# Eight products of constants on TensorE ahead of the turning of a layer norm's result

## The reference

```python
x = x + tanh(g_xattn[0]) * L0_xattn(_layernorm(x), ctx, ctx, mask, ...)   # attention, 16 heads      A0
x = x + tanh(g_ffn[0])   * L0_ffn(_layernorm(x), ...)                     # 8 experts, top 2         M0
x = x + tanh(g_xattn[1]) * L1_xattn(_layernorm(x), ctx, ctx, mask, ...)   # attention with biases    A1
x = x + tanh(g_ffn[1])   * L1_ffn(_layernorm(x), ...)                     # switched attention       SW
x = x + tanh(g_xattn[2]) * L2_xattn(_layernorm(x), ctx, ctx, ...)         # mLSTM                    ML
x = x + tanh(g_ffn[2])   * L2_ffn(_layernorm(x), ...)                     # quantised conv FFN       CF
x = x + tanh(g_xattn[3]) * L3_xattn(_layernorm(x), ctx, ctx, ...)         # one wide head, then FFN  WA
x = x + tanh(g_ffn[3])   * L3_ffn(_layernorm(x), ...)                     # 16 experts, top 4        M3
```

## Time and profile before

| | |
|---|---|
| median of three runs | 3420.51 us (3406.86 to 3446.26) |
| the profiled execution | 3412.93 us |
| its span, first to last instruction | 3410.8 us |
| TensorE busy | 2673.2 us, 78% |
| VectorE, ScalarE, GpSimd busy | 52%, 43%, 4% |
| mean granted TensorE clock | 0.789 of full |

### The profile page before, as it was taken

The page is one execution under the profiler, slowest core; times in us unless marked ns, Lnnn a source line. Parts: engine busy times, 40 slices in busy tenths (PEclk is TensorE's granted clock), DMA queues, the critical chain, the costliest instruction groups (busy, mean ns, idle before and its releaser), DMA issues.

```text
span 3410.8 us, 50340 instructions
## 1 busy us (share of the span) xinstructions
PE 2673.2 (78%) x18402; PEld 1795.5 (53%) x18402; DVE 1782.7 (52%) x6456; ACT 1466.3 (43%) x4498; POOL 138.9 (4%) x180
## 2 busy tenths in 40 slices
PE   5888688876888777887778877788778887788876
PEld 2556445654556544565445654456544564454644
DVE  4544654447544565444654347543565435744356
ACT  3363243632436324462344622446234462345622
POOL 0000000000000000000000000000000000000000
PEclk9896787876879678796788867888678886788867
DMA  2041000410004000040000500004000050000400
GB/s 118 1 100 38 7 10 1 100 38 13 4 1 115 23 13 4 7 113 18 14 2 7 118 13 14 2 7 118 13 15 2 7 118 13 15 3 19 109 10 4
DMA packets 311269, 114.93 MB, mean 34 GB/s; under 512 B 267712, under 2 KB 294336, under 8 KB 310768
## 3 DMA queue, kind: packets, MB, share of 16 engines
q1 hardware_dynamic: 311024, 111.72, 12.9%
HBM read 63.46 MB, written 48.23 MB: 33 GB/s over the span
## 4 chain that ended last, share of the span: by engine, by line
PE 55%; DVE 22%; ACT 14%; issue 5%; DMA 3%; POOL 1%; SPq 0%; DVEq 0%; ACTq 0%
PE banks L448 5%; ACT PP L772 5%; PE banks L392 5%; PE banks L327 5%; PE banks L641 3%; PE banks L514 3%; DVE nm L1087 3%; PE banks L541 3%; PE banks L330 2%; PE banks L291 2%; PE banks L601 2%; PE banks L339 2%; DVE xn L1044 2%; PE banks L487 2%; PE banks L415 2%
## 5 line engine op out<-in xcount | busy, mean ns | idle before, releaser
L772 ACT ACTIVATE PP<-banks,nm 128x128 f32<-128x128 f32 x1568 | 482.2, 380 | 226.4 <-DVE nm L1087 139.4
L1087 DVE TENSOR_REDUCE nm<-banks 128x8 f32<-128x1024 f32 (+1 forms) x208 | 240.8, 1161 | 514.6 <-PE banks L330 345.7
L780 ACT ACTIVATE PP<-banks 128x512 f32<-128x512 f32 (+1 forms) x400 | 236.5, 593 | 265.6 <-PE banks L392 258.2
L392 PE MATMUL banks<-w_sb,PP 128*128 128x128 f32 x1536 | 297.8, 328 | 33.5 <-ACT PP L772 27.0
L392 PEld LDWEIGHTS banks<-w_sb,PP 128*128 128x128 f32 x1536 | 207.0, 168 | 101.5 <-issue 46.3
L1629 POOL TENSOR_TENSOR rs<-mv,half 128x2 f32<-128x2 f32 x160 | 112.5, 703 | 2966.0 <-DVE mv L1024 2966.0
L514 PE MATMUL banks<-va,PP 128*128 128x64 f32 x1024 | 169.4, 318 | 50.8 <-ACT PP L780 41.1
L448 PEld LDWEIGHTS banks<-w_sb,qk 128*128 128x128 f32 x1280 | 193.3, 241 | 7.2 <-issue 3.1
L327 PE MATMUL banks<-qk,gs 32*128 32x512 f32 x512 | 185.7, 808 | 12.9 <-ACT PP L772 8.2
L448 PE MATMUL banks<-w_sb,qk 128*128 128x128 f32 x1280 | 192.5, 323 | 0.9 <-DVE qk L1222 0.9
L291 PE MATMUL banks<-w_sb,xn 128*128 128x128 f32 x288 | 79.0, 373 | 143.5 <-DVE xn L1044 118.9
(11 more groups left out here) (281 smaller groups left out, 5146.8 us busy)
## 6 DMA issues: line engine op xcount, KB each, us to landing
va<-v_d SPq DMA_DIRECT2D x32, 512.0 KB, 5.9
o_d<-oa SPq DMA_DIRECT2D x64, 256.0 KB, 2.1
va<-o_d SPq DMA_DIRECT2D x32, 512.0 KB, 3.9
pv_d<-PP SPq DMA_DIRECT2D x16, 512.0 KB, 4.3
oa<-pv_d SPq DMA_DIRECT2D x16, 512.0 KB, 4.3
v_d<-PP SPq DMA_DIRECT2D x16, 512.0 KB, 3.6
v_d<-tmp SPq DMA_DIRECT2D x16, 512.0 KB, 3.3
w_sb<-weights SPq DMA_DIRECT2D x1, 5603.0 KB, 22.4
```

The source lines that it names most:

```text
L392: e = pe.transpose(bank(k, 2)[:, cols(j)], P[k][:, 512 * (u % 2) + 128 * j:][:, 0:128], ident)
L772: e = act.activation(P[k][:, 512 * (u % 2) + 128 * j:][:, 0:128], bank_[:, cols(j)], ACT.Exp, bias=nm[k][:, m:m + 1], accum_out=ssum[k][:, ...
L780: act.activation(PT[k][:, 512 * (u % 2):512 * (u % 2) + maps * 128], bank(k, 2)[:, 0:maps * 128], ACT.Copy).then_inc(pT_ok[k], 1)
L1087: e = dve.tensor_reduce(m, b3(scores[:, 0:maps * 128], maps), AX.X, ALU.max, negate=True)
```

## The change

A new helper waits until x has been updated by the last stage and then runs eight bf16 products of 128x512: the identity `identb` is the stationary operand and `causb`, repeated four times, the moving one. They write the whole of the bank whose first half `pe_turn` overwrites directly afterwards. Nothing reads their result. The helper is called directly ahead of `pe_turn` in M0, A1, SW, ML, CF, WA and M3, in both lanes and all 8 turns: 7 x 2 x 8 = 112 times, 896 products. A0 and the second layer norm of WA are left as they are. Other engines' programs don't change.

```diff
+        def pe_idle_products(pe, k, i, stage, n):
+
+            pe.wait_ge(x_up[k], x_up.n(i, stage - 1))
+            for _ in range(8):
+                pe.matmul(bank(k, n), identb[:, :], bc(causb[:, :], 1, 4), start=True, stop=True, skip_group_check=True)
+
         def pe_turn(pe, k, i, j, src, n):
...
@@ pe_small_attention
             yield
+            if s:
+                pe_idle_products(pe, k, i, A1, 2)
             pe_turn(pe, k, i, (XN_A0, XN_A1)[s], xn[k], 2)
...
@@ pe_mixture0
             yield
+            pe_idle_products(pe, k, i, M0, 0)
             pe_turn(pe, k, i, XN_M0, xn[k], 0)
...
@@ pe_switched_attention
+            pe_idle_products(pe, k, i, SW, 0)
             pe_turn(pe, k, i, XN_SW, xn[k], 0)
...
@@ pe_mlstm
+            pe_idle_products(pe, k, i, ML, 0)
             pe_turn(pe, k, i, XN_ML, xn[k], 0)
...
@@ pe_conv_ffn
+            pe_idle_products(pe, k, i, CF, 0)
             pe_turn(pe, k, i, XN_CF, xn[k], 0)
...
@@ pe_wide_attention
+            pe_idle_products(pe, k, i, WA, 2)
             pe_turn(pe, k, i, XN_WA, xn[k], 2)
...
@@ pe_mixture3
+            pe_idle_products(pe, k, i, M3, 0)
             pe_turn(pe, k, i, XN_M3, xn[k], 0)
```

## The result

The changed kernel takes 3481.35 us (median of four runs, 3472.38 to 3496.68) against 3415.54 before: a ratio of 1.0174, with a 95% interval from 1.0109 to 1.024. It is slower, as forecast (3445), and inside the range, but by more: 66 us between the medians, where the forecast was 25 above the median known then. The profiled execution is the slowest of the four, 3496.68 us; its span is 3494.6 us, 83.8 more than that of the kernel before, where the prediction's sum had 33.

A forecast was written before the change was run, and what follows sets the result against it. TensorE, busy 78% of the span, was taken as nearest to the bound. Costs of 24.9 less gains of 19.8 gave 5.1 us in a turn, 41 in eight, four fifths 33; on 3412.93, 3446, said as 3445; range 3365 to 3530.

The forecast's parts named there:

- The wait on x_up costs nothing: In all fourteen places of a turn TensorE arrives after x was updated, so the new wait was costed at 0.
- The price of a product: Eight products take 1.7 us at full clock, 3.4 at half; beyond idle time, 24.9 us in a turn.
- The cover: TensorE's idle time before L291's transposes, 143.5 us, about 1 us per place, under which added products cost nothing.
- The products raise the clock: A set run at half leaves the clock at full, saving 19.8 us in a turn; mean clock 0.789 to about 0.85.
- Attention holds the clock: Behind A1 of lane 1, attention at half would run at full clock and stay there, saving 6.6 us in a turn.
- The places that I left out: Savings counted only for work right behind a set; A0 of lane 1 to M0 of lane 0 reckoned at +1.7 us.
- Four fifths of it reach the end: Later waits on TensorE may absorb delay or gain, so 33 of the 41 us in eight turns were taken.
- The first: Rival: the clock rises but attention behind A1 of lane 1 doesn't hold it; 75 us more, 3488; chance 0.22.
- The second: Rival: the products, multiplying constants, don't raise the clock, which stays at 0.79; 159 us more, 3572; chance 0.08.
- the third: Rival: CF, WA and M3 sets keep the clock full until the next set, above 0.9; 3358 us; chance 0.25.
- my own case: Products cost 24.9 us in a turn and the clock gives 19.8 back; 3400 to 3480 us, chance 0.45.

The follow-up runs named there:

- e6: The changed kernel with one product in place of eight in each of the 112 places, wait kept; 1.0026 against the kernel before.
- e3: The kernel before with the eight products in one place of a turn alone, A1 of lane 1; 0.9975 against the kernel before.
- e9: The changed kernel plus six quarter-array products ahead of the second output turning in A0 of lane 0, from the second turn on; 1.0353 against the kernel before.
- e10: The changed kernel plus six quarter-array products ahead of the first output turning in A0 of lane 0; 1.0199 against the kernel before, 3471.77 us.

## Why the prediction was right, and where it was off

- *The wait on x_up costs nothing.* Right: idle before the products 0.0, and e6 at 1.0026.
- *The price of a product.* Right: 1.73 and 3.39 us for a set, 1.7 and 3.4 reckoned. The clock at the place was not always as reckoned: the sets of A1 of lane 1 and of WA of lane 1 run at full (WA's was counted under the gains), and all sets cost 22 us in a turn beyond their cover, where 24.9 were put in.
- *The cover.* Right: of the 13.6 us of idle time in the fourteen places of the turn of the earlier trace rows, only the 0.68 before ML of lane 1 is still idle in the changed kernel's turn.
- *The products raise the clock.* Right in kind: M3 of lane 0 and WA of lane 1 show it, and quarter-array products in the same places give 1.0985 (e1). It gave less than I put in, some 15 us in a turn by the sum below and not 19.8, and the mean clock rose to 0.813 where I had named about 0.85.
- *Attention holds the clock.* It can, against the rule of the Trainium skill for transposes ("TensorE: Matmul & The Clock Gate", Part 4: PE-mode transpose) that the prediction weighed: −6.2 us reckoned as −6.6 (e3), at 1.00 in seven of eight turns. It does not always: in the changed kernel the clock falls once in that stretch (0.84), and about 4.4 us were gained behind the set of A1 of lane 1. That this row of the table came out near what was reckoned is luck: the set itself was reckoned at 3.4 us and the stretch that ends with it grew by nothing (−0.2), since its clock was higher too.
- *The places that I left out.* This is the step that was off most. The sum took for granted that "What that saves is the work right behind it", and that every other stretch keeps the clock it had. The stretch between A0 of lane 1 and M0 of lane 0 lost its full clock and cost 7.4 us in a turn where 1.7 were reckoned, 5.7 too little. All other stretches together came to +5.1, reckoned +3.4, with errors of both signs among them. So the one stretch is 5.7 of the 7.4 us by which the turn was off.
- *Four fifths of it reach the end.* Not borne out: the differences between the marks already contain whatever later waits absorb, and outside the one stretch they came to more than the full sum, not to less (+5.1 against +3.4). Turns 2 to 7 add up to 75 us, the start gives 1.5, the first turn 2 and the last 5.5, which makes the 83.8 of the profiled execution.
- *The rivals.* The first (attention doesn't hold the clock) gave 3488, near the measured 3481, by the wrong mechanism. It was a stretch without any change ahead of it that fell, not the one behind A1. The second (clock as before) and the third (above 0.9 and shorter turns) are out, with the clock at 0.813 and longer turns.

The sum that fits the profiled execution is thus: 22 us in a turn for the uncovered products (35.7 from set to transposes in the turn of the earlier trace rows, less 13.6 of cover), 5.7 lost by the clock where nothing was expected, and, as what then remains to 12.5, some 15 given back elsewhere. The 15 are not measured apart. The median, 3481, lies just above my own case (3400 to 3480); it is inside the range of 3365 to 3530 because the rivals, with other mechanisms, had widened it. That much is luck. The median of the runs is 15 us below that execution; which stretches fell in the runs without a trace stays open. It also stays open which of the thirteen other places add the last tenths of a us to the shift; only M3 of lane 1 was taken away alone.

## What to carry to other kernels

On a kernel that swings between the two clocks, price an added or moved burst in two sums: what it costs and saves on the spot, which rows give to some tenths of a us as long as the clock at the place stays what it was, and what the shift does to every later stretch that is at one clock by a narrow margin. List these stretches first (the same mixture at 1.00 in one place and 0.50 in another gives them away) and give the forecast a term for each. If products are to warm the clock, add them in few places with a long stretch behind them and test each alone; two places gave 0.988 here, three covered ones 1.004, fourteen 1.017.

## What was not expected of the hardware

- One group of full-array work raised the clock in all 63 turns in which it began up to 0.66 us after the clock's fall, and in none of the 21 in which it began 0.75 to 0.80 us after it.
- The same instructions took 18.6, 20.0, 26.0 or 33.6 us (A0 of lane 1 to M0 of lane 0, at 1.00, 1.00, 0.62 and 0.50), the last three with M0's eight products in them and the last with the delay of e9 too, and each value came back to 0.1 us in every turn of a trace from the second on.
- A delay of 2.7 us moved that stretch by −6.0 us in one place (e10) and by +7.6 in another (e9).
- Products of a quarter of the array (32 of 128 rows) take as long as full ones and don't hold the clock: 0.745 on average against 0.813 for the same number of full ones, and 0.789 without any.
